# Attention scores: one product of 128 query rows becomes four products of 32 query rows on separate columns of the array

## The reference, cut to what matters

```
scores = jnp.einsum('bqhd,bkhd->bhqk', q, k_all) * SCALE
scores = jnp.where(valid[:, None, None, :], scores, -1e+30)
probs = jax.nn.softmax(scores, axis=-1)
o = jnp.einsum('bhqk,bkhd->bqhd', probs, v_all)
```

## Time and profile before

| | us |
|---|---|
| median of 2 runs | 2340.1 (2339.66 to 2340.54) |
| span of the profiled execution | 2339.1 |
| TensorE matmul busy in it | 2311.7 (99%) |
| VectorE, ScalarE, GpSimd busy | 1488.0, 1356.3, 508.3 |
| `attend`, about | 579 to 1775 |

### The profile page before, as it was taken

The page is one execution under the profiler, slowest core; times in us unless marked ns, Lnnn a source line. Parts: engine busy times, 40 slices in busy tenths (PEclk is TensorE's granted clock), DMA queues, the critical chain, the costliest instruction groups (busy, mean ns, idle before and its releaser), DMA issues.

```text
span 2339.1 us, 48442 instructions
## 1 busy us (share of the span) xinstructions
PE 2311.7 (99%) x14320; PEld 1999.4 (85%) x14320; DVE 1488.0 (64%) x4154; ACT 1356.3 (58%) x4300; POOL 508.3 (22%) x538
## 2 busy tenths in 40 slices
PE   8999999998999999999999999999999999999998
PEld 7887777777999999999999999999998888888886
DVE  5899999983666666666666666666665344334433
ACT  4878888874666666666666666666665222222221
POOL 5211221211223333332222222222223011011101
PEclk9999999999999999999999999999999999999998
DMA  5344444448999999898998999999885333333331
GB/s 207 92 126 114 112 127 116 111 113 283 342 344 293 294 290 289 292 290 289 294 289 283 295 295 292 289 290 295 292 295 178 99 101 106 93 100 108 94 101 43
DMA packets 400360, 488.63 MB, mean 209 GB/s; under 512 B 63136, under 2 KB 334752, under 8 KB 397216
## 3 DMA queue, kind: packets, MB, share of 16 engines
q1 hardware_dynamic: 363296, 351.93, 49.3%
q0 software_dynamic: 36864, 134.23, 17.2%
HBM read 397.89 MB, written 88.08 MB: 208 GB/s over the span
## 4 chain that ended last, share of the span: by engine, by line
PE 77%; DVE 15%; issue 4%; SPq 1%; DMA 1%; DVEq 1%; ACT 0%; ACTq 0%
PE s_bank L1010 20%; PE o_bank L1022 19%; PE pt L1057 10%; DVE q_t L668 5%; PE proj L1509 5%; PE proj L1511 5%; PE proj L1510 5%; DVE part_s L659 5%; DVE q_t L684 5%; PE o_bank L1038 2%; PE slim L1540 1%; PE wide L1556 1%; PE wide L1551 1%; PE wide L1552 1%; PE turn L1530 1%
## 5 line engine op out<-in xcount | busy, mean ns | idle before, releaser
L977 DVE CUSTOM_DVE_ANT_0 probs<-s_bank,mask 128x544 f32<-128x544 f32 x512 | 371.1, 725 | 426.5 <-PE s_bank L1010 425.0
L931 ACT ACTIVATE probs<-probs,neg_max 128x544 f32<-128x544 f32 x512 | 383.9, 750 | 405.1 <-DVE neg_max L977 405.1
L1010 PE MATMUL s_bank<-k_t,q_t 128*128 128x288 f32 (+1 forms) x2048 | 558.3, 396 | 6.6 <-DMA q_t<-q_spill 4.4
L1022 PEld LDWEIGHTS o_bank<-p_t,v_c 128*128 128x128 f32 x4096 | 527.9, 192 | 28.8
L1022 PE MATMUL o_bank<-p_t,v_c 128*128 128x128 f32 x4096 | 540.1, 275 | 0.0
L1010 PEld LDWEIGHTS s_bank<-k_t,q_t 128*128 128x128 f32 x2048 | 351.2, 192 | 63.4 <-DMA q_t<-q_spill 4.8
L138 POOL DMA_INDIRECT v_c<-in_v_rows,v_row x256 | 255.2, 997 | 300.9 <-PE o_bank L1022 260.3
L1057 PE MATMUL pt<-ident,probs 128*128 128x128 f32 x2048 | 311.3, 275 | 0.0
L737 PE MATMUL acc<-w_hi,x_hi 128*128 128x512 f32 x764 | 304.6, 399 | 0.1
L903 ACT ACTIVATE p_t<-pt 128x512 f32<-128x512 f32 x512 | 295.9, 578 | 10.3 <-PE pt L1057 1.2
L738 PE MATMUL acc<-w_lo,x_hi 128*128 128x512 f32 x764 | 299.8, 392 | 0.0
(11 more groups left out here) (152 smaller groups left out, 3299.8 us busy)
## 6 DMA issues: line engine op xcount, KB each, us to landing
k_t<-in_k_pages SPq DMA_DIRECT2D x1024, 128.0 KB
q_spill<-wo_early SPq DMA_DIRECT2D x512, 64.0 KB, 1.8
q_t<-q_spill SPq DMA_DIRECT2D x64, 512.0 KB
o_spill<-o_t SPq DMA_DIRECT2D x64, 512.0 KB, 5.3
raw<-o_spill SPq DMA_DIRECT2D x64, 512.0 KB, 3.5
k_t<-in_w_qkv SPq DMA_DIRECT2D x11, 1024.0 KB, 5.7
v_spill<-wo_early SPq DMA_DIRECT2D x8, 1024.0 KB, 6.6
k_spill<-wo_early SPq DMA_DIRECT2D x128, 64.0 KB, 1.8
```

Of the source, the lines that this page charges most:

```text
L931: nc.scalar.activation(probs[:, j % SLOTS_P], probs[:, j % SLOTS_P], ACT.Exp, scale=-1.0, bias=neg_max[:, j % 2:j % 2 + 1], accum_out=row_ ...
L977: nc.vector.tensor_tensor_reduce(out=probs[:, j % SLOTS_P], in0=s_run, in1=mask[:, par], scale=-SCALE, scalar=3.0e38, op0=ALU.add, op1=ALU ...
L1010: last = pe.matmul(s_bank[:, columns].rearrange("p (s t) -> p s t", t=PSIZE), q_t[:, par, g], k_t[:, par, slots, g], start=True, stop=True)
L1022: last = pe.matmul(o_of(n), v_c[:, par, c, g * HD:(g + 1) * HD], p_t[:, i, c], start=g < QUAD and c == 0, stop=False)
```

## The change

In `score`, each of the two products of a unit is replaced by four. Product a takes the 32 query rows a * 32 to a * 32 + 31 as its stationary operand (128 x 32) and the same keys as before as its moving operand, and writes to partitions a * 32 to a * 32 + 31 of `s_bank`. An output that begins at partition a * 32 places the product on the 32 columns of the array that begin there. The semaphore is still raised once, by the last product.

```diff
                 for columns, slots in ((slice(BANK - CUT * PSIZE, BANK), slice(0, CUT)),
                                        (slice(BANK, BANK - CUT * PSIZE + KEYS), slice(CUT, NPP + 1))):
-                    last = pe.matmul(s_bank[:, columns].rearrange("p (s t) -> p s t", t=PSIZE), q_t[:, par, g],
-                                     k_t[:, par, slots, g], start=True, stop=True)
+                    for a in range(QUAD):
+                        rows = slice(a * S, (a + 1) * S)
+                        last = pe.matmul(s_bank[rows, columns].rearrange("p (s t) -> p s t", t=PSIZE), q_t[:, par, g, rows],
+                                         k_t[:, par, slots, g], start=True, stop=True)
                 last.then_inc(scored, 1)
```

## The result

The changed kernel takes 2500.3 us (median of 2 runs, 2498.56 to 2502.01) against 2340.1: 1.068 times the time, with a 95% interval of 1.065 to 1.071. A second comparison in another set of runs gave 2502.1 us and 1.069 (1.067 to 1.071). The profiled execution took 2502.0 us with a span of 2500.2, which is 161.1 us or 0.315 us per unit more than before.

The account below looks back on a forecast made before the run. TensorE was taken as the only bound. Side-by-side products add nothing and switching costs 0.36 us in each of 512 units, 184 us; 2339.1 + 184 = 2523 us of span, so 2524 us measured, range 2370 to 2620.

Parts of the forecast that it names:

- The bound: TensorE alone bounds the attention, busy 1195.1 of 1196.2 us, so time added there appears in full at the end.
- The products at no cost: In the scores, four narrow products run side by side: 0.92 us per unit as before, a change of nothing.
- The four terms: Cost per unit of getting in and out of the narrow scores: 0.33 to 0.40 us, taken as 0.36, 184 us.
- Entry: Time lost per unit going from a full-array transpose into the narrow scores: 0.10 us.
- Exit: Time lost per unit going from the last narrow scores back to full-array work: 0.11 us.
- Reload: Full-array weights loaded after the exit: 0.09 us, being 0.10 in three units of four and 0.06 in the fourth.
- First weights: First weight loads of the narrow scores, 32 columns per product with nothing hiding them: between 0.03 and 0.10 us.
- The free switch: Rival: switching columns at the scores is nearly free, only the 0.02 us stagger per unit; 2350 us, chance 0.09.
- Not side by side: Rival: the four score products overlap only partly or not at all; 2995 to 3937 us, chance 0.14.
- The strict order: Middle case: second records wait for first, next product behind them; scores 2.07 us, 3113 us, within the 0.14 chance.
- Instructions and covers at nothing: Extra TensorE records, their fetch, VectorE's slack, the stage's transfers and waits were to add no time.
- The marks named in advance: Expected profile signs: scores about 1.2 us, values 1.0, fours within 0.02; idle without a cause on TensorE meant wrong.

## Why the prediction was right

- **The bound.** Right. The time added on TensorE in the attention appeared whole at the end: 163 us by the chain, 161 in the span.
- **The products at no cost.** Right. Fours take 0.24 and 0.22 us, as single records did. The experiment on the same columns shows what they would have cost otherwise, 2.73 us per unit. The Trainium skill's rule that I had set against it, that a weight load overlaps running matmuls only where the row groups differ (TensorE: Matmul & The Clock Gate, What overlaps and what doesn't), does not hold inside a section of this trace: the narrow products share all their rows, and no load shows between one four and the next once the first weights are in (0.24 and 0.22 us).
- **The four terms.** That narrow columns would cost what rows cost was an assumption without a row of its own, and the runs bear it out. Entry 0.10, measured 0.09. Exit 0.11, measured 0.11. Reload 0.09 on average, measured 0.10 and 0.05, so 0.09. First weights: I took about 0.06, the middle of 0.03 to 0.10; it measured 0.02. This term carries most of the error. 512 x 0.04 is 20 us, the entry 512 x 0.01 another 5, together about the 24 us by which 2524 missed 2500. The row had shown 128 columns, and the cost goes with the columns (0.02, 0.05 and 0.10 us for 32, 64 and 128), the four loads going side by side. The low end of my bounds was the right choice; a quarter of 0.10 is 0.025, which I had rounded up to 0.03.
- **The free switch.** It failed at both ends at once: 0.11 us at the way in and 0.21 at the way out, each above the 0.09 from which it would have decided. The Trainium skill's span model for packed tiles (TensorE: Matmul & The Clock Gate, Measured speedup vs the span model) describes what happens inside a section (the stagger of the four, 0.02 us, against its 3 x 4 ns) and leaves out the way in and out, which here are all of the loss.
- **Not side by side.** Excluded by the records that start in fours. The strict order, its middle case, was excluded again by the swapped loops.
- **Instructions and covers at nothing.** Right in the sum. Nothing idle appeared on the matmul side, the clock stayed at 1.00, and the DMA share fell from 0.91 to 0.83 as the stage grew longer. Finer cuts on the whole array cost 12 us for 4 added pairs, so records of 128 columns do cost something (0.94 in place of 0.92 us); what is free is the narrow one that hides behind its three neighbours.
- **The marks named in advance.** The scores read 1.05 and the values 1.09, where I had written about 1.2 and 1.0. The chain starts a piece where the last one's columns end, so the exit stands partly with the values. The sum was right, the split was not. One mark did appear that I had written down as a sign of being wrong, idle without a cause, though on the weight-load side: 0.17 us at each way in. I had meant it for late instruction fetch. It is not that: one added narrow product per unit (two pairs) has such a wait in every unit, 156.9 us in 474 waits, and four added full-array pairs bring none.

## What to carry to other kernels

Cutting a full product into narrow ones that run side by side wins nothing where the full product already costs only its streamed columns, and every stretch of such products costs one way in and one way out, 0.3 us here, whether it holds two narrow matmul records or sixteen. Before using a part of the array, count how often the order of the program changes between parts and the whole, multiply, and gather the partial products into as few stretches as possible. If the kernel already has one such stretch, its neighbours' start distances give the price beforehand; here they gave 0.36 us where 0.32 was measured.

## What the runs showed that I had not expected

- Four streams read the same 128 partitions at once with no loss: 0.24 and 0.22 us per four, as for one stream.
- Narrow float32 records start in another order than that of the program: with four records in a row on the same columns, fours on different columns still started together, 13 ns or so apart in place of 7 (0.04 and 0.02 us over the four).
- One product of 32 query rows against 32 keys on its own costs 0.36 us of TensorE time, more than the sixteen narrow records of a whole score add (0.31).
